# A graph attention layer: a short scan of the softmax maximum's chain moves ahead of uT in VectorE's order

## What is computed

```python
h = relu(layernorm(x))
xm = h @ W_n2m.T;  ea = rbf @ W_r2m.T
xl = xm @ Wl.T + bl;  xr = xm @ Wr.T + br          # 8 heads of 16
u = leaky_relu(xl[src] + xr[dst] + ea @ We.T, 0.2)
logits = einsum('ehd,hd->eh', u, att)
mx = segment_max(logits, dst)
p = exp(logits - mx[dst])
alpha = p / segment_sum(p, dst)[dst]
out = segment_sum(xl[src] * alpha, dst) + bias
return x + out @ W_m2n.T
```

## Time and profile before

| what | us |
|---|---|
| median of the runs shown | 2429.84 |
| lowest and highest of these 3 runs | 2429.38, 2435.47 |
| the profiled execution, its own time | 2429.01 |
| its span in the trace | 2426.8 |
| PE busy in the span | 2250.9 |
| DVE busy | 1483.2 |
| ACT busy | 1438.3 |
| POOL busy | 1721.3 |
| TensorE's granted clock over the span, share of full speed | 0.98 |

### The profile page before, as it was taken

The page is one execution under the profiler, slowest core; times in us unless marked ns, Lnnn a source line. Parts: engine busy times, 40 slices in busy tenths (PEclk is TensorE's granted clock), DMA queues, the critical chain, the costliest instruction groups (busy, mean ns, idle before and its releaser), DMA issues. The chain is left out here.

```text
span 2426.8 us, 71198 instructions
## 1 busy us (share of the span) xinstructions
PE 2250.9 (93%) x16556; PEld 1731.1 (71%) x16557; DVE 1483.2 (61%) x4174; ACT 1438.3 (59%) x4331; POOL 1721.3 (71%) x1914
## 2 busy tenths in 40 slices
PE   3968999999999999999999999999999999999977
PEld 2745777777777777777777777777677777777756
DVE  4734666656665666566656665666566656666676
ACT  2714666656665666566656666666566656666653
POOL 3777777777777777777777777777777777777401
PEclk9989999999999999999999999999999999999999
DMA  6243443444444444444444444444444334444117
GB/s 199 80 109 96 103 104 97 98 100 107 98 99 102 106 98 99 102 104 99 100 101 105 99 100 101 106 99 99 100 104 99 100 100 106 99 99 98 45 51 123
DMA packets 288519, 244.84 MB, mean 101 GB/s; under 512 B 168503, under 2 KB 259608, under 8 KB 287826
## 3 DMA queue, kind: packets, MB, share of 16 engines
q1 hardware_dynamic: 221726, 116.00, 21.1%
q0 software_dynamic: 60704, 120.20, 19.8%
q10 hardware_dynamic: 5652, 3.68, 0.5%
HBM read 228.23 MB, written 19.40 MB: 102 GB/s over the span
## 5 line engine op out<-in xcount | busy, mean ns | idle before, releaser
L778 POOL DMA_INDIRECT xl_g<-xl_table,src_tab x1708 | 1636.2, 958 | 522.9 <-issue 514.4
L999 DVE SCALAR_TENSOR_TENSOR uT<-banks,relu 128x256 f32<-128x256 f32 x854 | 347.3, 422 | 536.6 <-issue 513.4
L860 PE MATMUL banks<-msg,onehot 128*128 128x177 f32 x3416 | 634.4, 328 | 7.2 <-DVE acc L955 2.9
L860 PEld LDWEIGHTS banks<-msg,onehot 128*128 128x128 f32 x3416 | 518.7, 191 | 170.8 <-issue 153.6
L898 ACT ACTIVATE distance<-iota_n,minus_slot 128x128 f32<-128x128 f32 x1708 | 541.1, 390 | 0.0
L813 PE MATMUL banks<-ident,xl_g 128*128 128x128 f32 x3416 | 464.3, 280 | 31.4 <-DMA xl_g<-xl_table,src_tab 31.3
L813 PEld LDWEIGHTS banks<-ident,xl_g 128*128 128x128 f32 x3416 | 445.4, 202 | 37.9 <-DMA xl_g<-xl_table,src_tab 37.8
L913 ACT ACTIVATE relu<-banks 128x256 f32<-128x256 f32 x854 | 315.8, 383 | 144.2 <-PE banks L813 115.8
L794 PE MATMUL banks<-onehotT,xr_parts 128*128 128x256 bf16 x2562 | 355.8, 275 | 22.5 <-issue 17.3
L903 ACT ACTIVATE onehot<-distance 128x512 f32<-128x512 f32 x427 | 269.0, 630 | 116.8 <-PE banks L860 105.3
L907 ACT ACTIVATE rbfT<-banks 128x128 f32<-128x128 f32 x427 | 116.5, 273 | 352.9 <-PE banks L808 347.4
(11 more groups left out here) (193 smaller groups left out, 1643.5 us busy)
## 6 DMA issues: line engine op xcount, KB each, us to landing
slot_bc<-slot_dram SPq DMA_DIRECT2D x427, 128.0 KB
xl_g<-xl_table,src_tab POOLq DMA_INDIRECT x1708
rbf<-in_edge_attr SPq DMA_DIRECT2D x854, 32.0 KB
masks<-masks_dram SPq DMA_DIRECT2D x864, 12.1 KB
out<-in_x SPq DMA_DIRECT2D x16, 336.0 KB
out<-result POOLq DMA_DIRECT2D x6, 896.0 KB, 9.3
xl_table<-lr_sb SPq DMA_DIRECT2D x49, 64.0 KB, 1.5
xl_in<-xl_table SPq DMA_DIRECT2D x7, 448.0 KB, 4.9
```

The lines of the kernel that those rows point to most:

```text
L778: pool.indirect_dma_start(out=xl_g[:, k % RING, t], out_offset=None, in_=xl_table, in_offset=bass.IndirectOffsetOnAxis(ap=src_tab[:, e:e + ...
L860: mm = nc.tensor.matmul(U_ps[h], onehot[:, j % 2, t], msg[:, j % 2, t], start=i == 0, stop=i == PT - 1)
L999: nc.vector.scalar_tensor_tensor(out=uT[:, s % 2, h * PIECE:(h + 1) * PIECE], in0=z_ps[h], scalar=SLOPE, in1=relu[:, h], op0=ALU.mult, op1 ...
```

## The change

The copy of 8 numbers and the forward scan of CHAIN are issued between `msg` and `uT` of the same step, where they stood behind `uT`. The backward scan and what follows stay behind `uT`. No instruction is added or dropped, the waits stay with their instructions, and no other engine's order changes.

```diff
@@ -991,6 +991,13 @@
                     nc.vector.tensor_copy(to[:, :, :, D_HEAD:HC], wm_ps[:, :, row]).then_inc(msg_ready, 1)
+                b = batch_at(s, r, CHAIN)
+                if has(b):
+                    found, old = by_head(seq_in[:]), by_head(seq_max[:, (s - CHAIN) // BATCH % 2])
+                    nc.vector.tensor_copy(found[:, :, 0:1], old[:, :, SEQ - 1:SEQ]).then_inc(seq_ready, 1)
+                    dve.wait_ge(seq_ready, 3 * b + 3)
+                    nc.vector.tensor_tensor_scan(seq_forth[:], seq_cut[:, 0:HEADS * SEQ], seq_in[:], -BIG, ALU.add,
+                                                 ALU.max).then_inc(seq_half, 1)
                 if inside(k, STEPS):
@@ -1016,11 +1023,7 @@
                 b = batch_at(s, r, CHAIN)
                 if has(b):
                     par = (s - CHAIN) // BATCH % 2 ^ 1
-                    found, old, new = by_head(seq_in[:]), by_head(seq_max[:, 1 - par]), by_head(seq_max[:, par])
-                    nc.vector.tensor_copy(found[:, :, 0:1], old[:, :, SEQ - 1:SEQ]).then_inc(seq_ready, 1)
-                    dve.wait_ge(seq_ready, 3 * b + 3)
-                    nc.vector.tensor_tensor_scan(seq_forth[:], seq_cut[:, 0:HEADS * SEQ], seq_in[:], -BIG, ALU.add,
-                                                 ALU.max).then_inc(seq_half, 1)
+                    old, new = by_head(seq_max[:, 1 - par]), by_head(seq_max[:, par])
                     dve.wait_ge(seq_half, b + 1)
```

## The result

The changed kernel is slower by a third of a per cent: 2440.92 us median of 17 runs (2434.5 to 2445.28) against 2432.88 us of the kernel before in 17 runs next to them, ratio 1.0034, interval 1.0028 to 1.0041. That is +8.0 us where I had put +1.7. The time lies within the stated range; the forecast of no change did not come true, since the interval excludes it.

The account below looks back on a forecast made before the run. POOL's row of gathers was taken to bound the edge loop: 2429.0 profiled, 0 for PE's 34 us, 0 for the end, +2 for gathers gave 2431.0; with 0.8 for the median 2431.8, written as 2431.5; range 2423 to 2441.

Parts of the forecast that it names:

- the forecast of no change: Whole kernel: time within 7.3 us of 2429.84, about 0.3%; chance 0.78.
- PE's wait of 34.7 us goes whole: PE at L808 waits for DVE's L955: the 0.68 us wait in the chain step vanishes, with 0.35 us to spare.
- The pair ahead of `uT` is covered: DVE's copy and forward scan, 0.9 to 1.0 us, fit the 1.34 us of idle time ahead of `uT`; cost 0.
- The gain turns into waits for gathers and none of it arrives: POOL's 39.96 us a batch stay, so PE's 34 us turn into waits of L813 for `xl_g`; 0 gained.
- The last step offers nothing: At the edge loop's end PE already waited for its gather, 2.72 us after the issue; 0, up to +2.
- What the move does to the gathers: +2 us: New starts of the chain's two scans on DVE change how much POOL's gathers are lengthened: +2 us, between -7 and +12.
- kept phases: Gathers keep their places against the chain's scans: the two scans cost 15.9 us in place of 7.1, +8.8 us.
- the mean over all phases: Every phase between gathers and scans equally frequent: 0.08 us a scan, 8.5 us for two scans in 52 batches, +1.4.
- The other scans lose their fixed phase, -2 to +2: Scans outside the chain's two, carrying the remaining 17 us of the gathers' excess, shift against the gathers: perhaps -2 or +2.
- the rival of the collisions: The chain's scans on DVE fall on gathers more often, 0.2 to 0.44 us a hit; over 7.3 us slower, chance 0.13.
- Its price for both scans of each batch hit, 2450: Forward and backward scan of each batch both lengthen a gather, at 0.23 to 0.39 us: some 2450 us, outside the range.
- The rule of the Trainium skill, page "SBUF — State Buffer", section "Who interferes with whom": A VectorE instruction with two SBUF inputs contends with a GpSimd instruction reading SBUF; the one that comes second blocks.

Follow-up runs that it names:

- the moved copy: The kernel before with only the copy of 8 numbers moved ahead of `uT`, the forward scan staying behind: 2432.3 us, ratio to before 0.9994.
- the padded kernel: The changed kernel with PE turning the attributes four times more than needed in the step behind each chain: 2439.88 us, ratio to before 1.0025.

## Why the prediction was right or wrong, step by step

- *PE's wait of 34.7 us goes whole.* Right: 0.5 us are left.
- *The pair ahead of `uT` is covered.* Right: 0.55 us of idle time remain where 0.35 to 0.45 were forecast (the copy starts before the last `msg` row has ended, 2063.65 against 2063.74), and `uT` starts 1.16 us behind L813.
- *The gain turns into waits for gathers and none of it arrives.* Right: 31.3 us of such waits became 61.9, and with three gathers a step the same reorder brings 39 us.
- *The last step offers nothing.* Right: 2.72 and 2.74 us from the last gather to L813.
- *What the move does to the gathers: +2 us.* This is the step that failed. The mechanism was right, and no other was found at work; the term was mis-sized: +8.4 us in the profile, +8.0 in the medians. I had the sum for kept phases, 15.9 us for the two scans and +8.8 in all, and threw it away with the argument that at a faster pace PE would slide through all phases, so that the mean over all phases, 8.5 us, would hold. Measured are 16.0 us for the two scans. The phases did move, forward 8.7 where the kept phases said 5.5 and backward 7.4 where they said 10.4, but they never became evenly spread: evenly spread phases would hit one of the scans in 0.9 / 1.25 of the chains, 37 of 52, and 50 had a hit. A gather that is held up moves all those behind it, so I think that the hits themselves steer the phase; no run shows it. In before, the phase stood on a near miss in many chains: the gather of the earlier trace rows starts 0.07 us ahead of the forward scan. Counted again over all 52 chains of the trace by the same rule, kept phases give 14.5 us and not 15.9, so +7.3: still far nearer than +1.4.
- *The other scans lose their fixed phase, -2 to +2.* Right in sum, -0.5 us: RAISE's two steps lost 4.2 us and all else 1.2, `onehotT` gained 3.8, BACK's scan 1.0.
- *Chances.* What came is the rival of the collisions, which had 0.13 and said that it goes past 0.3% where nearly every batch has a hit of middling size, 0.28 us a batch. Measured: 50 hits in 52 chains, 0.32 us each. The prediction's own sign for it was a mean gather of 963 ns or more, and it is 963. With the sum of kept phases beside me I should have given it about a half; the forecast of no change rested on an argument for which no row spoke. Its price for both scans of each batch hit, 2450, comes to 2455 by its own 0.23 and 0.39 us (52 x 0.62 - 7.1 over 2429.84), and no chain of the trace had both; and its upper bound for the gathers' term stands as +12 in one place and +11 in another.
- *The rule of the Trainium skill, page "SBUF — State Buffer", section "Who interferes with whom".* For the instructions with two SBUF inputs it held, and the runs with `seq_cut` and `forth` in PSUM agree with it. The prediction's sentence that only the scans with two SBUF inputs lengthen a gather was too narrow: RAISE's steps, `onehotT` and the clears of `acc` do too, and 16.7 of the 23.8 us of before lie outside the chain. The size isn't the wait to the scan's end either: 0.51 us less the distance, where the scan takes 0.70. That 0.51 is the scan's end as the gather sees it was the prediction's reading, which no run tests. Used as a tool, the rule would have pointed to the gain that the reorder missed.

What stays open is why the gathers settle where they do. Kept phases gave nearly the right sum for the changed kernel and a wrong one for the moved copy (3 to 8 us expected, none found), so that the first was partly luck. How much of the changed kernel's loss belongs to PE's pace is open too: the padded kernel brought back only part of the old pace.

## What to carry to other kernels

Ask first which engine works from its first to its last instruction without a wait, not which is busiest: here PE was busy for 93% of the time and did not bound the edge loop, while POOL, 71% busy by the page, issued a gather every 1.25 us from one end to the other. Before moving an instruction on an engine with slack, look at what it shares with the engine that has none; through that alone can the move change the time, and here it lost. And where such a row is disturbed a little by each of several instructions, take the disturbance away (here, one input to PSUM) and don't count on a mean over its phases.

## What the runs showed of the hardware that I had not expected

A gather issued from 0.05 to 0.5 us behind the start of one of the chain's scans with both inputs in SBUF ends later by 0.51 us less that distance, within 0.02 us, in all three pairs shown and in the 80 hits of the two traces; the same forward scan with one input in PSUM adds nothing in 29 meetings. Two addresses, `seq_cut` and `forth`, were worth 20 us of 2433, out of 23.8 us of excess that the gathers had in before. The bf16 instruction that makes `onehotT` also lengthens gathers, by 0.05 to 0.16 us where they meet, 1.4 us in all before and 5.2 after. So does the clearing of `acc`, which reads nothing, but only in its last three of seven parts: the three gathers that met these in before ended 0.95 or 0.96 us after the part's end, as if they had begun only then, also the one that was issued 0.11 us ahead of it, while two issued 0.12 and 0.19 us behind the start of earlier parts took 0.94. Why the parts differ is open.
